# The MLP phase of a hybrid layer: another order of the FFNs, and search steps placed as one stream by due date

## The reference

```python
x = x + attention(layernorm(x))                 # 32 heads of 16, causal
x = x + ffn(layernorm(x))                       # int4-like weights, groups of 128, I = 1792
x = x + sparse_mlp(layernorm(x))                # I = 1376
x = x + ffn(layernorm(x))                       # the same weights again

# ffn:        (silu(x @ gate) * (x @ up)) @ down
# sparse_mlp: s = silu(x @ w_gate.T); the k = 688 entries of a row that are smallest
#             in absolute value are set to 0 (ties by index); (s * (x @ w_up.T)) @ w_down.T
```

## Time and profile before

| | us |
|---|---|
| median of 3 runs | 2173.3 (2172.37 to 2176.78) |
| the profiled execution | 2174.31 |
| its span, first to last instruction | 2172.5 |
| PE busy | 2016.4 (93%) |
| DVE busy | 1556.7 (72%) |
| ACT busy | 1019.6 (47%) |
| POOL busy | 551.5 (25%) |

### The profile page before, as it was taken

The page is one execution under the profiler, slowest core; times in us unless marked ns, Lnnn a source line. Parts: engine busy times, 40 slices in busy tenths (PEclk is TensorE's granted clock), DMA queues, the critical chain, the costliest instruction groups (busy, mean ns, idle before and its releaser), DMA issues.

```text
span 2172.5 us, 38409 instructions
## 1 busy us (share of the span) xinstructions
PE 2016.4 (93%) x14288; PEld 1234.3 (57%) x14288; DVE 1556.7 (72%) x2736; ACT 1019.6 (47%) x1658; POOL 551.5 (25%) x587
## 2 busy tenths in 40 slices
PE   5887999999999987899999999999999988889989
PEld 2342344444444345677677677677677665656756
DVE  6665677777777332279878778778788799898951
ACT  3221365565565621156356355355364464645611
POOL 2223454743532332111211111111112111111221
PEclk9897799999999988999999999999999999999999
DMA  7666235432333063020310310410400402122000
GB/s 260 230 211 178 73 94 134 126 93 68 93 84 95 21 217 146 27 79 1 105 53 2 124 53 1 138 40 1 161 17 1 166 2 105 53 97 70 11 10 11
DMA packets 115657, 187.35 MB, mean 86 GB/s; under 512 B 43201, under 2 KB 68177, under 8 KB 115521
## 3 DMA queue, kind: packets, MB, share of 16 engines
q1 hardware_dynamic: 91344, 133.22, 19.7%
q0 software_dynamic: 9088, 32.12, 5.1%
q10 hardware_dynamic: 15088, 20.19, 2.6%
HBM read 151.59 MB, written 33.62 MB: 85 GB/s over the span
## 4 chain that ended last, share of the span: by engine, by line
PE 45%; DVE 13%; issue 3%; ACT 1%; POOL 1%; DVEq 0%; ACTq 0%; POOLq 0%
PE ga L1364 10%; PE ub L1364 10%; PE acc L1374 10%; DVE junk L1536 5%; PE acc L1416 5%; PE ga L1392 4%; PE ub L1392 4%; DVE pat L1540 2%; DVE h L1593 1%; PE d_tr L1213 1%; DVE kept L1581 1%; PE d_tr L1403 1%; DVE T L1542 0%; DVE junk L1571 0%; POOL pp L1331 0%
## 5 line engine op out<-in xcount | busy, mean ns | idle before, releaser
L842 DVE TENSOR_REDUCE mx<-s 128x1 f32<-128x512 f32 (+3 forms) x608 | 380.6, 660 | 126.8 <-PE s L731 73.2
L1467 ACT ACTIVATE kept<-ax,T 128x1376 f16<-128x1376 f32 x248 | 357.0, 1440 | 123.7 <-DVE T L1542 115.4
L823 ACT ACTIVATE pr<-s 128x1024 f32<-128x1024 f32 (+3 forms) x352 | 300.9, 868 | 241.4 <-PE s L750 179.3
L1536 DVE TENSOR_SCALAR_CACHE_REDUCE junk<-ax,T 128x1376 f16<-128x1376 f32 x248 | 406.4, 1639 | 3.2
L1326 POOL TENSOR_TENSOR lohi<-h,lohi 128x256 f16<-128x256 f32 x224 | 165.2, 738 | 874.6 <-ACT lohi L1478 874.5
L1364 PE MATMUL ga<-xT_f,w_gate 128*128 128x256 f16 x2688 | 332.9, 274 | 19.8 <-DVE h L1593 16.8
L1364 PE MATMUL ub<-xT_f,w_up 128*128 128x256 f16 x2688 | 331.8, 274 | 0.0
L1374 PE MATMUL acc<-w_down,lohi 128*128 128x512 f16 x1344 | 326.2, 379 | 1.5 <-POOL lohi L1326 1.5
L1364 PEld LDWEIGHTS ga<-xT_f,w_gate 128*128 128x128 f16 x2688 | 262.4, 98 | 96.6 <-DVE h L1593 25.3
L1364 PEld LDWEIGHTS ub<-xT_f,w_up 128*128 128x128 f16 x2688 | 263.9, 98 | 31.4
L728 PE MATMUL s<-K,Q 65*128 65x512 f16 (+3 forms) x768 | 245.0, 344 | 26.1 <-DMA K<-onerow 13.0
(11 more groups left out here) (142 smaller groups left out, 2416.2 us busy)
## 6 DMA issues: line engine op xcount, KB each, us to landing
ring<-wgu_scr SPq DMA_DIRECT2D x64, 688.0 KB, 5.3
ring<-wd_scr SPq DMA_DIRECT2D x24, 768.0 KB, 4.7
wgu_scr<-tk_h POOLq DMA_DIRECT2D x16, 344.0 KB, 6.4
q_scr<-qk_h ACTq DMA_DIRECT2D x16, 256.0 KB, 4.0
k_scr<-qk_h ACTq DMA_DIRECT2D x16, 256.0 KB, 2.5
v_scr<-v_f ACTq DMA_DIRECT2D x16, 256.0 KB, 2.7
Q<-q_scr SPq DMA_DIRECT2D x32, 128.0 KB
K<-k_scr SPq DMA_DIRECT2D x32, 128.0 KB
```

The costliest lines, as they stand in the source:

```text
L823: nc.scalar.activation(pr[:, kb % 2, j0:j1, 0:w], scores, ACT.Exp, scale=SCALE).then_inc(e2_ok, 1)
L842: nc.vector.tensor_reduce(dst, s1[u % 2][:, 0:(j1 - j0) * w].rearrange("p (j k) -> p j k", k=w), AX.X, ALU.max).then_inc(r1_ok, 1)
L1467: nc.scalar.activation(kept[1][:, :], ax[k % 2][:, 1, :], ACT.Sign, scale=-1.0, bias=TF[:, 1:2], accum_out=cnt[:, 1:2]).then_inc(c1_ok, 1)
L1536: nc.vector.tensor_scalar(junk[:, :], ax[k % 2][:, 0, :], TF[:, 0:1], -float(KZERO), ALU.is_lt, ALU.add, accum_out=cnt[:, 0:1]).then_inc(c ...
```

## The change

It has three parts.

**The order.** `mlp_order` now gives two FFNs to each period except 3 and 6 (`FFN_ALONE`), which get one. The FFNs come in the sequence f1 1, f1 2, f1 3, f2 0, f1 4, f2 1, f1 5, f2 2, f1 6, f2 3, f1 7, f2 4, f2 5, f2 6. The gates of chunk k+1 stay behind the FFNs of period k, and `down k` follows them.

| window | FFNs before | FFNs after |
|---|---|---|
| 0 | f1 1, f1 2 | f1 1, f1 2 |
| 1 | f1 3, f2 0 | f1 3, f2 0 |
| 2 | f1 4, f2 1 | f1 4, f2 1 |
| 3 | f1 5, f2 2 | f1 5 |
| 4 | f1 6, f2 3 | f2 2, f1 6 |
| 5 | f1 7 | f2 3, f1 7 |
| 6 | f2 4 | f2 4 |
| 7 | f2 5, f2 6 | f2 5, f2 6 |

**The items.** All items form one list. At each slot the planner takes the highest rate that any chunk's due date still asks for (work left up to it by span left up to it), adds span times rate to a budget that is held at 6000 at most, subtracts the slot's own DVE work, and places items while the budget covers half of the next one's cost. An item of chunk k still can't stand before the end of `gates k`.

What the planner then writes, as the number of items in the eight slots of the down at the head of a window, and where the items end:

| windows | down, before | down, after | last item, before | last item, after |
|---|---|---|---|---|
| 1 | 0 1 0 1 0 1 0 1 | 2 1 1 0 1 0 0 1 | gates, slot 5 | FFN 2, slot 13 |
| 2 | 0 1 0 1 0 1 0 1 | 2 1 1 0 1 0 1 0 | gates, slot 5 | FFN 2, slot 11 |
| 3 | 0 1 0 1 0 1 0 1 | 2 1 1 1 1 0 1 1 | gates, slot 5 | gates, slot 5 |
| 4 | 0 1 0 1 0 1 0 1 | 2 1 1 0 1 0 0 1 | gates, slot 5 | FFN 2, slot 13 |
| 5 | 1 1 0 1 1 1 0 1 | 2 1 1 0 1 0 1 0 | gates, slot 5 | FFN 2, slot 11 |
| 6 | 1 1 0 1 1 1 0 1 | 2 1 1 1 1 0 1 1 | gates, slot 5 | gates, slot 5 |
| 7 | 1 0 1 0 1 0 1 0 | 2 1 1 0 1 0 0 1 | FFN 2, slot 11 | FFN 2, slot 11 |

**The sign pass.** Its elementwise result, which nobody reads, goes to kept[0] instead of kept[1], so the first pass of chunk k waits for the first mask of chunk k-1 only. In an FFN slot the sign pass of item 0 no longer stands ahead of the high part.

```diff
-                    wait(act, hm_ok, TPC * k)
+                    wait(act, hm_ok, TPC * k - 1)
                 wait(act, p_ok, NBITS * k + i)
-                nc.scalar.activation(kept[1][:, :], ax[k % 2][:, 1, :], ACT.Sign, scale=-1.0, bias=TF[:, 1:2],
+                nc.scalar.activation(kept[0][:, :], ax[k % 2][:, 1, :], ACT.Sign, scale=-1.0, bias=TF[:, 1:2],
...
                         silu(s, n)
-                        for k, i in bits[:1]:
-                            signs(k, i)
+                        if bits and bits[0][1]:
+                            signs(*bits.pop(0))
                         high(s, n)
-                        bits = bits[1:]
...
+FFN_ALONE = (3, 6)
...
-    order = [("f1", 0), ("gates", 0), ("f1", 1), ("f1", 2), ("gates", 1), ("down", 0)]
-    for k in range(1, NC - 3):
-        order += [("f1", k + 2), ("f2", k - 1), ("gates", k + 1), ("down", k)]
-    order += [("f1", NC - 1), ("gates", NC - 2), ("down", NC - 3)]
-    order += [("f2", NC - 4), ("gates", NC - 1), ("down", NC - 2)]
-    return order + [("f2", NC - 3), ("f2", NC - 2), ("down", NC - 1), ("f2", NC - 1)]
+    ffns = [("f1", 1), ("f1", 2)]
+    for k in range(NC - 3):
+        ffns += [("f1", k + 3), ("f2", k)]
+    ffns += [("f2", NC - 3), ("f2", NC - 2)]
+    order = [("f1", 0), ("gates", 0)]
+    for k in range(NC):
+        first, second = ffns[0], ffns[1] if k not in FFN_ALONE else None
+        ffns = ffns[1 if second is None else 2:]
+        order += [first, second, ("gates", k + 1)]
+        order.append(("down", k))
+    return [s for s in order if s and s != ("gates", NC)] + [("f2", NC - 1)]
...
+    first, last = at["gates", 0] + 1, at["down", NC - 1]
+    own = [(p, slot, spans[s.kind], evictions[s.kind] + 700 * len(slot.taken) + 1800 * len(slot.stats)
+            + 1100 * len(slot.scaled) + 1400 * len(slot.lows))
+           for p, s in enumerate(stages[first:last], first) for slot in s.slots]
+    items = [(k, n) for k in range(NC) for n in range(len(costs))]
+    budget = 0
+    for n, (p, slot, span, duty) in enumerate(own):
+        rate = 0
+        for k in range(NC):
+            ahead = [(l, d) for q, _slot, l, d in own[n:] if q < at["down", k]][:-2]
+            left = sum(costs[item] for c, item in items if c <= k)
+            if left and ahead:
+                rate = max(rate, (left + sum(d for _l, d in ahead)) / sum(l for l, _d in ahead))
+        budget = min(budget + span * rate - duty, 6000)
+        while items and p > at["gates", items[0][0]]:
+            k, item = items[0]
+            left = sum(q < at["down", k] for q, _slot, _l, _d in own[n:])
+            if budget < costs[item] // 2 and left > 3:
+                break
+            slot.items.append(items.pop(0))
+            budget -= costs[item]
+    assert not items
```

## The result

The changed kernel takes 2199.3 us (median of 6 runs, 2188.6 to 2206.1), the kernel before 2174.9 on the same chip (6 runs, 2172.4 to 2185.5). The ratio is 1.0086 with a 95% interval of 1.0055 to 1.0117. The profiled execution took 2191.28 us with a span of 2189.4; the prediction had 2190.3 and 2188.5 for these, and 2189.3 for the median.

What follows compares the result with a forecast made beforehand. PE was taken to bound two-FFN windows and DVE's search one-FFN windows. Terms 13.4 + 2.0 - 0.6 + 1.2 gave +16.0 us, a median of 2189.3; range 2174 to 2202, the forecast case's own 2183 to 2196.

Steps and rivals of the forecast that it cites:

- Two early steps in down: Downs before windows 1, 2, 4, 5: two search steps in slot 0 delay PE's turns; 3.35 us each, +13.4.
- Single windows: One-FFN windows, now 3 and 6: later FFN start, fewer steps in FFN slots, later pp in gates; together -0.6 us.
- Window 7: Its down grows from 19.77 to 21.82 us with the new early steps: +2.0.
- Finishing in FFN slots: Windows 1, 2, 4, 5: scan, mask and passes now fall into FFN slots; 0.3 us each, +1.2.
- such collisions: DVE scans beside POOL low parts, sharing an SBUF port: if four windows lose what window 7 loses, total 3.6 us more.
- The clock as a rival: PE's clock falls in five to seven new downs, about 2.5 us each: +12 to 18, 2201 to 2207; chance 10%.
- the sum of 16.0: Whole span: 13.4 + 2.0 - 0.6 + 1.2 us, taking it from 2172.5 to 2188.5.
- The mask's wait: First sign pass's 1.58 us wait for POOL's mask goes in two downs behind single windows; no separate gain, already counted.
- The median: Time of the whole kernel: 2189.3 us, 0.74% slower than the 2173.3 shown before.

Runs made afterwards that it cites:

- Cleared downs: The changed kernel, but downs before two-FFN windows take items only in slots 1, 3, 5, 7, one each: 2189.7 us, ratio 1.0044.
- single steps: The changed kernel, but with at most one item in any down slot before a two-FFN window: ratio 1.0051, MLP phase 1340.7 us.
- the filler: The changed kernel plus eight unused matmuls behind the first product of downs 0 to 6, in PE's wait for turn 3: ratio 1.0061.

## Why the prediction was right, point by point

- *Two early steps in down, +3.35 each for windows 1, 2, 4 and 5, 13.4 in all.* Right in mechanism and size: 2.54 us of wait at turn 3 for a low part behind the two steps, +3.33 in windows 1 and 4, and the same in 2 and 5 once the clock is held (162.02). Cleared downs give 158.70 back, single steps 161.0.
- *Single windows, -0.6.* The two together went from 239.5 to 239.1, -0.4. FFN at +22.99 against the predicted +23.0. Behind the down, the waits for h went from 8.1 to 6.3 us; those for pp from 2.0 to 2.6, where I had taken 1.2 more.
- *Window 7, +2.0.* The window grew by 2.1 (129.2 to 131.3, from the first transpose of down 6 to that of down 7), but not in the way given. The down cost its 2.0 (+21.78 with the filler); 1.1 more came by the clock, and 1.0 went because only 0.2 us of the waits in the earlier trace rows was left in its FFNs.
- *Finishing in FFN slots, +1.2.* Wrong: 0. PE has no wait for h or POOL's low part in windows 1, 2, 4 and 5. Window 7 of before was the nearest row but not a fitting one. POOL's low part took up to 2.87 us in windows 1, 2, 4 and 5 as well, beside DVE's scans of 3.0 us, but PE uses it two slots later. So the 3.6 us that the prediction gave for such collisions did not come.
- *The clock as a rival, 10%, 2.5 us in five to seven downs.* The step that failed: I set an all-or-none event against the forecast. The clock fell in four of seven downs, 1.1 us each where PE bounds, nothing in window 6, where DVE does: 3.0 in all. The price of 2.5 a fall was mis-sized too. Added up (rounded), the phase shows 13.3 in the four downs, 2.2 of clock in windows 2 and 5, 2.1 in window 7, -0.4 in the single windows and -0.4 outside windows 1 to 7. The clock took the room of the finishing term and of window 7's gain, so the sum of 16.0 stands near 16.7 partly by luck: errors cancel. The Trainium skill (TensorE: Matmul & The Clock Gate, section Why this matters for your kernels) wants no PE-idle gaps above about 3 us; here two gaps of 1.62 and 2.54 with matmuls between were enough in four downs of seven, and the measurement decides.
- *The mask's wait.* I said that its effect was inside the new positions. It was, but by the placement, not by the edit of the sign pass, as its removal shows. Where the old plan is kept, the edit is worth 0.8 us in down 6.
- *The median.* 2199.3 against 2189.3. The phase was 0.7 from the prediction. The rest lies, by the profiles, in the part ahead of it, a program that the change leaves alone. The six executions follow the granted clock: 0.967 at 2188.6 and 2191.3 us, 0.958 at 2206.1. What makes the clock stay low for longer in some of them was not tried.

## What to carry to other kernels

Work of another engine that is hidden in one stage can stand in the way in the next: look at how far ahead the bounding engine is in each stage, and keep filler items out of the slots where it is one eviction ahead. A planner that levels work by due dates could gain nothing here while work could not cross the windows: even with its downs cleared the phase was 6.6 us longer than before. With the gates moved and the slots around the downs kept clear it was 17.3 us shorter, 0.8% of the time (the ratio of the times has 1.1%). Where a program has a noisy part that the change doesn't touch, compare the part that it does.

## What the runs showed of the hardware

PE's granted clock fell from 2.4 to 1.2 GHz after idles of 1.62 and 2.54 us, with 2.1 us of matmuls between. Eight matmuls (1.89 us) in the second of these idles kept it at 2.4 GHz in all seven downs and saved 3.0 us over the phase. With equal waits it fell in downs 1, 4, 5 and 6 and not in 0, 2 and 3, in both profiles of the changed kernel, and in downs 1 and 3 alone with the old order of FFNs. Equal idles therefore don't settle whether it falls; what does was not found. A single idle of 1.99 us in an FFN was once enough, and one of 1.86 in the same place was not. After 1.62 and 1.12, as in down 5 of before, it never fell.

POOL's low part of 128x256 took 0.67 us as a rule and up to 2.87 beside a scan of DVE (3.0 us).
